# A third pair of input buffers in the feed-forward passes, and the second pair of tiles normalised before the down projection

## What is computed

```python
def layer0(x):                                   # x: (8, 2048, 1024)
    x = x + mamba(layernorm(x), W_in, conv_w, W_x, W_dt, b_dt, W_Bp, D_param, W_out)
    x = x + ffn(layernorm(x), w_gate, w_up, w_down)
    x = x + attn(layernorm(x), W)                # causal, K and V from W, q = its own input
    x = x + ffn(layernorm(x), w_gate, w_up, w_down)   # the same weights again
    return x

def ffn(x, w_gate, w_up, w_down):                # int weights, scaled by 1/127
    gate = x @ (w_gate / 127).T                  # 1024 -> 3072
    up   = x @ (w_up / 127).T
    return (silu(gate) * up) @ (w_down / 127).T  # 3072 -> 1024
```

## Time and profile before

| what | us |
|---|---|
| median of 2 runs | 3257.29 (3256.41 to 3258.16) |
| the profiled execution | 3256.57 |
| its span, core 3 (the slowest) | 3255.0 |
| spans of the eight cores | 3236.7 to 3255.0 |
| TensorE matmul busy, core 3 | 1988.5 (61% of the span) |
| VectorE, ScalarE, GpSimd busy | 963.6, 730.7, 361.6 |

### The profile page before, as it was taken

One profiled execution on the slowest core, in us unless ns is written; L12 is line 12 of the kernel. 1 busy time (PEld: TensorE's weight loads), 2 busy tenths in 40 slices (PEclk: granted clock), 3 DMA queues, 4 the chain that ended last, 5 costly groups with the idle time before them and its releaser, 6 DMA issues.

```text
span 3255.0 us, 29917 instructions; the slowest of 8 cores (3236.7 to 3255.0 us)
## 1 busy us (share of the span) xinstructions
PE 1988.5 (61%) x9432; PEld 970.6 (30%) x9432; DVE 963.6 (30%) x1612; ACT 730.7 (22%) x1163; POOL 361.6 (11%) x420
## 2 busy tenths in 40 slices
PE   0355555555555542864958668316986676769687
PEld 0233333333333311321423223113443232324242
DVE  3233444444344452102212121353432121212121
ACT  0244445454454530100101011110010201101010
POOL 0212212222222243021000000000000000000000
PEclk9677676766767665886998889758998798989899
DMA  7300000000000058243030211452132412030303
GB/s 240 91 14 25 2 26 1 26 1 26 26 1 26 1 175 280 82 133 136 8 107 16 65 65 39 139 167 73 40 110 95 148 48 75 26 104 13 116 1 101
DMA packets 69852, 233.32 MB, mean 72 GB/s; under 512 B 8450, under 2 KB 8578, under 8 KB 67652
## 3 DMA queue, kind: packets, MB, share of 16 engines
q10 hardware_dynamic: 38016, 124.80, 11.2%
q1 hardware_dynamic: 27460, 91.92, 9.3%
q0 software_dynamic: 4224, 14.68, 1.1%
HBM read 170.55 MB, written 60.82 MB: 71 GB/s over the span
## 4 chain that ended last, share of the span: by engine, by line
PE 38%; DMA 20%; DVE 13%; ACT 9%; issue 8%; DVEq 4%; POOLq 3%; POOL 3%; ACTq 2%; SPq 0%
PE ps_s L1032 16%; DMA arena<-wd_c 6%; PE ps_s L998 5%; DVEq L143 4%; DMA arena<-xs 3%; PE ps_s L1102 3%; PE ps L1102 3%; POOLq L143 3%; ACT L683 2%; PE ps_s L1355 2%; POOL arena L564 2%; DVE arena L520 2%; PE ps L764 2%; DMA arena<-wu_t 2%; PE ps_s L1281 2%
## 5 line engine op out<-in xcount | busy, mean ns | idle before, releaser
L1032 PE MATMUL ps_s<-arena 128*128 128x512 bf16 x2304 | 510.2, 385 | 6.3 <-DVE arena L332 6.3
L588 PE MATMUL ps_s<-arena 128*128 128x256 bf16 x1024 | 209.5, 392 | 349.8 <-ACT arena L512 347.1
L322 PE MATMUL ps<-arena 128*128 128x128 bf16 x512 | 63.5, 308 | 472.8 <-DVE arena L311 472.8
L1032 PEld LDWEIGHTS ps_s<-arena 128*128 128x128 bf16 x2304 | 228.0, 99 | 287.1 <-issue 23.7
L1102 PE MATMUL ps_s<-arena 128*128 128x512 bf16 x768 | 211.1, 397 | 139.0 <-DMA arena<-wd_c 91.8
L269 ACT ACTIVATE arena<-arena 128x1024 bf16<-128x1024 f32 x64 | 67.7, 1057 | 895.2 <-DMA arena<-xs 786.5
L588 PEld LDWEIGHTS ps_s<-arena 128*128 128x128 bf16 x1024 | 135.3, 136 | 417.3 <-issue 366.6
L503 PE MATMUL ps_s<-arena 128*128 128x256 bf16 x1024 | 167.6, 335 | 112.4 <-DVE arena L451 64.8
L1047 DVE TENSOR_TENSOR arena<-arena,ps_s 128x512 bf16<-128x512 f32 x144 | 99.1, 688 | 421.6 <-ACT arena L1041 421.6
L1102 PE MATMUL ps<-arena 128*128 128x512 bf16 x768 | 210.8, 398 | 0.0
L998 PE MATMUL ps_s<-arena 128*128 128x512 bf16 x768 | 173.8, 390 | 51.4 <-ACT arena L1008 49.3
(11 more groups left out here) (91 smaller groups left out, 2354.4 us busy)
## 6 DMA issues: line engine op xcount, KB each, us to landing
xs<-arena ACTq DMA_DIRECT2D x48, 512.0 KB, 2.9
arena<-xs ACTq DMA_DIRECT2D x48, 512.0 KB, 4.3
arena<-wd_c SPq DMA_DIRECT2D x84, 256.0 KB, 2.6
arena<-wd_c ACTq DMA_DIRECT2D x84, 256.0 KB, 2.6
arena<-wg_t SPq DMA_DIRECT2D x16, 768.0 KB, 5.1
arena<-wu_t SPq DMA_DIRECT2D x16, 768.0 KB, 12.8
arena<-x ACTq DMA_DIRECT2D x16, 512.0 KB, 4.2
arena<-w_in ACTq DMA_DIRECT2D x8, 1024.0 KB, 10.6
```

Of the source, the lines that this page charges most:

```text
L322: lambda e, s=xn_bf_tile, dj=dj, pbf=pbf: e.transpose(pbf[:, dj * P:(dj + 1) * P], s[:, dj * P:(dj + 1) * P], g_ident),
L588: lambda e, dj=dj, ci=ci, bkx=bkx, half=half, par=par: e.matmul(psb[bkx][:, half * TCM:(half + 1) * TCM], win_bf[:, dj * 4096 + ci * P: dj ...
L1032: lambda e, hi=hi, dj=dj, bk=bk, par=par, wsrc=wsrc: e.matmul(psb[bk], wsrc[:, dj * H + hi * P: dj * H + (hi + 1) * P], fxnt[par][:, dj * ...
```

## The change

Tiles 2 and 3 get a third pair of buffers, fxC, in the former staging area, and now alternate as tiles 0 and 1 do. The loads of tiles 2 and 3 for chunk c wait for the stores of chunk c - 2 instead of c - 1 (for chunk 1: for the last weight conversion in pass 1, for the attention's end in pass 2). In the five turns the call for tiles 2 and 3 moves to the middle of the chunk, directly behind the one for tiles 0 and 1 and ahead of the down projection. In the turn after chunk 0 of pass 1 both calls stay where they are. Nothing is computed anew or left out.

```diff
+            fxC = [VA(F_STG, 4096, F32), VA(F_STG + 4096, 4096, F32)]
+
             def fxt(c, tt):
-                if pre and c == 0 and tt >= 2:
-                    return fxB[tt - 2]
-                if c % 2 == 1 and tt < 2:
+                if tt >= 2:
+                    if c == 0:
+                        return fxB[tt - 2] if pre else fxA[tt]
+                    if pre:
+                        return fxA[tt] if c % 2 == 1 else fxC[tt - 2]
+                    return fxC[tt - 2] if c % 2 == 1 else fxA[tt]
+                if c % 2 == 1:
                     return fxB[tt]
                 return fxA[tt]
@@ in f_ln_tiles, the waits of the loads of tiles 2 and 3
                             if c == 0:
                                 w += region["xin"]
+                            elif c == 1:
+                                if first:
+                                    w.append(prev_cast[0])
+                                else:
+                                    w += region["xin"]
                             else:
-                                w.append(mk_fst_chunk[c - 1])
+                                w.append(mk_fst_chunk[c - 2])
@@ between gate/up and down
                 if c + 1 < NKF and not (first and c == 0):
                     f_ln_tiles(c + 1, [0, 1], 8)
+                    f_ln_tiles(c + 1, [2, 3], 10)
@@ after the stores
-                if c + 1 < NKF:
-                    if first and c == 0:
-                        f_ln_tiles(c + 1, [0, 1], 8)
+                if c + 1 < NKF and first and c == 0:
+                    f_ln_tiles(c + 1, [0, 1], 8)
                     f_ln_tiles(c + 1, [2, 3], 10)
```

## The result

| what | before | after |
|---|---|---|
| median of all runs | 3257.83 us (10 runs) | 3189.85 us (11 runs) |
| the profiled execution | 3256.57 | 3190.49 |
| spans of the eight cores in it | 3236.7 to 3255.0 | 3161.8 to 3189.0 |

The ratio after to before is 0.9789, with a 95% interval of 0.9777 to 0.9801: 2.1% less, some 68 to 69 us, with the 2% line just inside the interval, so whether it is over 2% (for which the prediction gave 0.76) stays undecided. The prediction was 3184 us, 73 us less. Medians here hold a few runs in which one half of the chip was disturbed; the ratios leave them out.

A forecast was written before the change was run, and what follows sets the result against it. TensorE was taken to bound the kernel, idling in serial layer-norm chains between stages. Turns -113.4, middles +50.3 and clock -9.9 sum to -73.0 us, from 3257.3 to a forecast of 3184 us, range 3174 to 3199.

The forecast's parts named there:

- The turn: Five turns between chunks: stores, loads and layer norm leave the chain, gate/up starts 1.53 us in; 113.4 us saved.
- The middle: Five middles before down: the second pair adds 10.05 us each, its loads nearly hidden; 50.3 us added.
- The queue behind it: ScalarE's queue in the middle: first odd down weight issued about 10 us later, still 5.3 us ahead of down; no cost.
- The late first Silu: Gate/up behind each turn: store issues delay the first Silu some 0.3 us; 0.3 us a turn if cover were gone.
- The clock: Gate/up behind the five turns starts at 2.4 GHz instead of 1.2 after the shorter pause; 9.9 us saved, bounds 0 and 9.9.
- the two rows on which the step leaned: Clock reads 1.00 over a turn's first 1.64 us and over the 1.9 us pause before the last chunk's down projection.
- The sum: Whole kernel: -113.4 + 50.3 - 9.9 = -73.0 us, giving 3184 us, 2.2% less.
- A: Gate/up behind the turns: the clock gives nothing back, it still starts at 1.2 GHz; 3194 us; chance 0.11.
- B: Middles: the second pair costs its whole chain, 13.8 us instead of 10.05; 19 us more, 3203 us; chance 0.09.
- C: Five gate/up stages: denser work lowers the clock to 13/16; 95 us more, 3279 us; chance 0.03.
- D: Middles: moved loads still wait for a late store, adding a store's round trip; given no chance of its own.

The follow-up runs named there:

- the two runs on the middle: Changed kernel without layer norm and transposes of tiles 2 and 3 in five middles: 0.9629; with all four loads issued first: 0.9843; ratios to the kernel before.
- the best version: Changed kernel with both pairs' loads ahead of gate/up and layer norm steps inside its loop, the sixth turn included: ratio 0.9360 to the kernel before.

## Why the prediction was right, step by step

1. *The turn.* 1.53 us were predicted, 1.44 measured in each of 40 (five on eight cores). Right.

2. *The middle.* 10.05 us were taken from the one place where both pairs followed each other. 9.90 in the trace after, 10.0 to 10.3 by the growth of the five middles, 10.4 by leaving the work out. Right in size and in reason: a chain of VectorE, ScalarE and TensorE steps, with the loads under it.

3. *The queue behind it.* The odd weights kept their 5.3 us. The late first Silu was mis-sized, 1.8 to 2.6 us late and not 0.3, since the table load of 1.28 us was left out; what it cost TensorE was still only 0.4 us on core 2, nothing on core 3 and at most 1.1 us in the five turns of any core, inside the bound of 5 x 0.3.

4. *The clock.* 9.9 us predicted. The row of gate/up on the slowest core went from 510.2 us of busy time to

```profile
L1043 PE MATMUL ps_s<-arena 128*128 128x512 bf16 x2304 | 501.0, 381 | 9.6 <-DVE arena L1130 8.1 <-DVE arena L332 1.1 <-DVE arena L1058 0.4
```

with the same 2304 matmuls; over all cores the mean fell from 508.8 to 499.9, 8.9 us. Right, and the run that waits for the store shows cause and effect the other way round. But the two rows on which the step leaned were weaker than they were read: both show the clock inside a pause, and it reads 1.00 there even where it falls right behind (below). A pause of 1.85 us before a down projection is not safe, in the kernel before neither. That the clock holds over the turn's 1.44 us was shown only by the changed kernel; neither row could tell it beforehand, so that part of the step was luck.

5. *The sum.* 73 predicted, 68 to 69 measured by the ratio. The mean of the eight spans, over the runs that the ratio counts, says the same: 3242.7 us for the kernel before (13 runs, beside the experiments), 3174.0 for the changed one (9 runs). The 73 us are the five turns, five middles and the clock. In the segments one turn with its clock gives 23.3 us (pass 1) and 24.2 (pass 2), where 22.7 + 2.0 = 24.7 were predicted. The missing 4 us lie in small terms, most of them held at zero by the sum: 1.0 of the clock term, 0.4 for the late Silu, and the down projections. From first matmul to first addition the eight of them are 4.5 us longer in sum (520.6 to 525.1, mean over the cores), with 0.9 us more of matmul busy time (385.3 to 386.2) and 2.2 us more of waiting for down weights (90.3 to 92.5). The five experiments that change nothing inside a down projection read 518.6 to 524.1 there, so most of this can be scatter between profiles; its cause is not shown.

The rivals. A (no clock gain) is refuted by the 40 windows at 1.00. B falls to the two runs on the middle. C, the lower clock in answer to denser work, did not show: in the best version core 2 is busy for 265.6 of 300 us in pass 2, the other seven 265 to 269, and all eight are granted 0.98 or 0.99. The limiter of the Trainium skill (TensorE: Matmul & The Clock Gate, Seeing it yourself), 13/16 for a die of which three cores run dense matmuls, shows in no profiled execution of these kernels: their clock records hold only the levels 1.00 and 0.50, on every core. D falls with the loads being issued at once in the middle.

## What to carry to other kernels

A pause at which an in-order TensorE waits for a serial chain costs that chain's whole length; moving a piece of the chain from one pause to another pays only by what it overlaps with there (here 23 us of a turn became 10 in a middle), and a freed buffer alone pays almost nothing (4 us). The larger gain lies in cutting the chain into steps and placing each, in every engine's list, behind work that runs anyway: that took a middle of some 26 us to 1.9. Price a moved piece from a place in the trace where it already follows the same neighbour.

## What the runs showed of the hardware that was not expected

A pause of 1.85 us between gate/up and down, in the best version, was followed in 24 of 48 cases by a fall to 1.2 GHz within the first 3 us of down (granted 0.57 to 0.88 over them); the pause itself still read 1.00. In the run before it (both pairs inside gate/up) it was 34 of 48. After pauses of 1.16 to 1.19 us in the best version (16 cases) and after the turns of 1.44 us in the changed kernel (40 cases) it stayed at 1.00. One case, core 2, the pause and what follows it:

```profile
2825.20:2827.05 1.85, 0.00 (x1) 1.00 0.02 6
2827.05:2832.00 4.95, 4.69 (x12) 0.66 0.24 63
```

So that the clock reads 1.00 in a pause says nothing about the microseconds after it. In the kernel before, the same pause was looked at once, and that one gave the wrong comfort: it stands before the last down projection of both passes, and on 4 of the 16 occasions on the eight cores the first 3 us behind it read 0.85 to 0.87. One of the four is on the same core 3, in pass 1:

```profile
2000.02:2001.87 1.85, 0.00 (x1) 1.00 0.00 0
2001.87:2004.87 3.00, 2.71 (x8) 0.86 0.32 93
```

Whether the length of the pause decides it is not shown: behind these pauses stands a down projection that soon waits for its weights, behind the turns a dense gate/up. Nor is a pause of 1.44 us followed by a full clock in every place. In the best version the sixth turn (pass 1, chunk 0) has that length too, and on core 5 the clock had already fallen to 0.50 in the down projection ahead of it; over the 8 us behind the turn it read 0.79, on the seven other cores 1.00:

```profile
1498.13:1504.13 6.00, 5.13 (x12) 0.50 0.27 108
1504.13:1505.57 1.44, 0.00 (x1) 0.50 0.00 0
1505.57:1513.57 8.00, 8.00 (x30) 0.79 0.73 262
```
